# Moving the bias of three attention layers from TensorE to VectorE in a graph network kernel

## The chip, the cores and the metric

The kernel runs on one core of one Trainium2 chip. The metric is device time in microseconds for one execution, the median of several runs. The core has five engines that run their own instruction queues and wait for each other by semaphores: TensorE (PE in the profile; PEld is its loading of weights), VectorE (DVE), ScalarE (ACT), GpSimd (POOL) and SyncE (SP), which here only starts transfers.

## The reference

There are 50000 nodes with 128 features and 12500 edges, sorted by target. Two blocks follow each other: one convolution over the edges, then four attention layers, of which each does, with `x` the rows of the nodes:

```python
def _gat_layer(x, src, dst, ea, W, We, a_s, a_d, a_e, b, g, beta):
    h = x @ W
    e = ea @ We
    alpha = h @ a_s
    alpha = alpha[src] + (h @ a_d)[dst] + e @ a_e
    alpha = jax.nn.leaky_relu(alpha, NEG_SLOPE)
    alpha = _segment_softmax(alpha, dst, N)
    out = jax.ops.segment_sum(h[src] * alpha[:, None], dst, num_segments=N) + b
    mu = out.mean(-1, keepdims=True)
    var = ((out - mu) ** 2).mean(-1, keepdims=True)
    return (out - mu) * jax.lax.rsqrt(var + LN_EPS) * g + beta
...
for l in range(L):          # L = 4
    x = _gat_layer(x, src_f, dst_f, ea_f, W[l], We[l], att_src[l], ...)
```

A node without an incoming edge has only its own loop, so its row needs no other row. The kernel treats such rows apart ("dense" work) from those that edges touch.

## The kernel before, in words

Everything is fp32 unless said. The program is a sequence of blocks; in each, every engine has its own list, and all engines meet at the end of a block. After the set-up and a convolution block, four pairs follow: a dense block (`dense`, the rows no edge touches) and `attention(l)` for l = 0 to 3. The diff touches the second block of `attention`, for l = 0, 1, 2; the last layer (`final`) keeps its way of working. It also touches the set-up.

The attention block for a layer works over the edges, 125 at a time, two such groups (columns of `S` and `T`) to a **unit**: `NU` = 50 units. `S` holds the rows of the sources, `T` those of the targets, both [125, 100 or 101, 130]: 128 features and two score columns. For unit n, with ring place r = n % 4:

- `mask` (VectorE) multiplies the 0/1 matrices `M` by the attention weights into `MA`; `diagonal` (GpSimd) does the same with the identity into `DGB`. `diagonal(n)` may start when `aggregate(n-4)` is done.
- `aggregate` (TensorE) sums `S` rows by `MA` and `T` rows by `DGB` into bank r (8 passes, since an fp32 product is two passes). `copy_t` (ScalarE) takes the result to `XT`.
- `turn` (TensorE) transposes the two `S` tiles into bank 4+r (2 passes); `copy_s` (VectorE) takes them to `XT`.
- `multiply_t` and `multiply_s` (TensorE): a product of three rows of bf16 (`BR`, the bias split into three parts) with ones, 260 columns, puts the bias into the bank (L1698), and two fp32 products with the layer's weights, 130 columns, 4 passes, are added to it (L1702).
- `squares` (ScalarE) reads the rows from the banks and sums their squares, `root` takes the square root, `invert` (VectorE) the reciprocal, and `rescale_t`, `rescale_s` (VectorE, L1811 and L1818) multiply the rows in the banks by it and write them to `T` and `S`.
- `edge` (VectorE) keeps two columns of a unit for the rows that span two groups.

The order on an engine is written by hand: for slot t = 0 to 54, the operations of the list run one after the other, each for unit t minus its lag. SyncE stores ten pieces of `T` as their units get ready.

Of the kernel before, what the change touches and what calls it, by code (L numbers as in the profile page):

```python
# [11 lines left out]
D = 128  # L12
# [20 lines left out]
def gnn_kernel(nc, x, src, dst, ea, ew, w0, b0, wg, we, att_s, att_d, att_e, bg, gamma, beta, out):  # L33
    ctx = ExitStack()
    with ctx:
# [73 lines left out]
        BR = sb("BR", [3, L + 1, W], BF16)  # L109
        GC = sb("GC", [D, L])  # L110
# [513 lines left out]
        with nc.Block() as block:  # L624
# [7 lines left out]
            def _(dve):  # L632
# [18 lines left out]
                ch.add(nc.vector.tensor_copy(WIS[:, :], banks[6][0:P, 0:C]))  # L651
                dve.wait_ge(s_tab, 1)
# [71 lines left out]
            def _(pe):  # L724
                seg = segbox[0]
                carries(pe, seg, [(0, ("total", run[:, :])), (1, ("spread", lg[:, :]))])
                pe.wait_ge(s_vt, 1)
# [98 lines left out]
        def dense(first_group, groups, moves, move, arrive):  # L826
# [10 lines left out]
                "turned2_copied", "beta_added")  # L837
# [397 lines left out]
        def conv_layer():  # L1235
# [5 lines left out]
                "residual_added", "beta_added", "counted2", "variance2", "root2", "inverse2", "scale2",  # L1241
# [293 lines left out]
        def attention(l):  # L1535
# [80 lines left out]

            (masked, diag_ready, gathered, agg_copied, edged, agg_done, turned, turned_copied, next_done, squared,
# [10 lines left out]
            with nc.Block() as block:  # L1628
# [44 lines left out]
                def _(pe):  # L1673
                    def aggregate(n):
                        pe.wait_ge(*masked.at(n + 1))
                        pe.wait_ge(*diag_ready.at(n + 1))
                        r = n % NS
                        if n >= NS:
                            pe.wait_ge(*t_ready.at(n - NS + 1))
                        for a in range(2):  # L1680
                            o = banks[r][:, a * P:(a + 1) * P]
                            nc.tensor.matmul(o, S[:, 2 * n + a, 0:D], MA[:, r, a, :], start=True, stop=False,  # L1682
                                             skip_group_check=True)
                            ins = nc.tensor.matmul(o, T[:, 2 * n + a, 0:D], DGB[:, r, a, :], start=False, stop=True,  # L1684
                                                   skip_group_check=True)
                        ins.then_inc(gathered.s, 1)

                    def turn(n):
                        r = n % NS
                        if n >= NS:  # L1690
                            pe.wait_ge(*s_ready.at(n - NS + 1))
                        transposes(banks[4 + r], [S[:, 2 * n + a, 0:D] for a in range(2)]).then_inc(turned.s, 1)

                    def multiply(bank, xt, copied, done):
                        def op(n):
                            r = n % NS
                            pe.wait_ge(*copied.at(n + 1))
                            nc.tensor.matmul(product(banks[bank + r], 2 * P), ones3[:, 0:P],  # L1698
                                             BR[:, l:l + 1, 0:cols].broadcast_to([3, 2, cols]), start=True, stop=False,
                                             skip_group_check=True)  # L1700
                            for a in range(2):
                                ins = nc.tensor.matmul(product(banks[bank + r], 2 * P)[:, a, :],  # L1702
                                                       XT[:, r, xt + a * P:xt + (a + 1) * P], WCX[:, l, 0:cols],
                                                       start=False, stop=True, skip_group_check=True)
                            ins.then_inc(done.s, 1)
                        return op

                    multiply_t, multiply_s = multiply(0, 0, agg_copied, agg_done), multiply(4, 2 * P, turned_copied, next_done)
                    for t in slots:
                        run_slot(t, NU, [(0, aggregate), (1, multiply_t)] if final else [(0, turn), (0, aggregate), (1, multiply_t), (0, multiply_s)])  # L1710
# [13 lines left out]
                def _(act):  # L1724
# [8 lines left out]
                    def squares(n):  # L1733
                        r = n % NS
                        act.wait_ge(*agg_done.at(n + 1))
                        for a in range(2):
                            ins = nc.scalar.activation(Y[:, r, a, :], product(banks[r], 2 * P)[:, a, 0:D], ACT.Square,  # L1737
                                                       scale=D ** -0.5, accum_out=ss4[:, r, a:a + 1])
                        if not final:
                            act.wait_ge(*next_done.at(n + 1))  # L1740
                            for a in range(2):
                                ins = nc.scalar.activation(Y[:, r, 2 + a, :], product(banks[4 + r], 2 * P)[:, a, 0:D],
                                                           ACT.Square, scale=D ** -0.5, accum_out=ss4[:, r, 2 + a:3 + a])
# [8 lines left out]
                    for t in slots:  # L1752
                        run_slot(t, NU, [(3, root), (1, copy_t), (2, squares)])
# [8 lines left out]
                def _(dve):  # L1762
# [27 lines left out]

                    def invert(n):
# [4 lines left out]
                    def rescale_t(n):  # L1796
# [14 lines left out]
                        nc.vector.tensor_tensor(T[:, 2 * n:2 * n + 2, :], product(banks[r], 2 * P),  # L1811
# [3 lines left out]
                    def rescale_s(n):  # L1815
                        r = n % NS
                        dve.wait_ge(*inverted.at(n + 1))
                        nc.vector.tensor_tensor(S[:, 2 * n:2 * n + 2, :], product(banks[4 + r], 2 * P),  # L1818
# [3 lines left out]
                    for t in slots:  # L1822
                        run_slot(t, NU, [(0, diagonal), (0, mask), (4, rescale_t), (3, invert), (1, edge)] if final else [(0, mask), (4, rescale_s), (4, rescale_t), (0, copy_s), (3, invert), (1, edge)])
# [24 lines left out]
            for sig in (turned, turned_copied, next_done, s_ready):  # L1848
# [34 lines left out]
```

## Time and profile before

| | us |
|---|---|
| median of 3 runs (lowest, highest) | 2285.7 (2283.72, 2287.53) |
| the profiled execution, its own time | 2294.79 |
| its span, first to last instruction | 2293.1 |
| PE busy | 1745.7 (76%) |
| DVE busy | 1609.0 (70%) |
| ACT busy | 1513.0 (66%) |
| POOL busy | 1151.3 (50%) |

No engine is busy for the whole span, since the blocks differ. What a change inside one block is worth has to be read from that block: which engine has no gap there, and what the others wait for. In a timeline row the first number is the start in us from the span's start, the second how long the row's instructions took; what stands in brackets is how long the engine had been idle and what released it. Records of one engine can overlap a little, since an instruction's start is taken while the one ahead drains: the distance from one start to the next (the **pitch** below) is what an instruction costs on a full engine. A row of busy time by stretch has the stretch and its length, then for PE, PEld, DVE, ACT and POOL the busy time with the number of instructions, then TensorE's granted clock (1.00 is 2.4 GHz, 0.50 is 1.2 GHz), the share of the DMA engines and GB/s.

### The profile page before, as it was taken

The numbers are of one execution on the slowest core, as the hardware profiler recorded it, in microseconds if no ns is written. First come the engines' busy times: TensorE is split into PE (matmuls) and PEld (weight loads), VectorE is DVE, ScalarE is ACT, GpSimd is POOL, SyncE is SP. The second block draws the span as 40 slices with busy tenths as digits, with TensorE's granted clock in tenths as the row PEclk, the third lists the DMA queues.
The fourth block names the chain that finished last, engine by engine and source line by source line (L and its number), as shares of the span: only waits on it lengthen the run. The fifth ranks groups of instructions, "written<-read, shape, count | busy, mean of one in ns | idle before, by whom it ended". The sixth has DMA issues, their size and how long they took to land. (4 is left out here: it accounts for less than half of the span.)

```text
span 2293.1 us, 41415 instructions
## 1 busy us (share of the span) xinstructions
PE 1745.7 (76%) x9894; PEld 1277.6 (56%) x9894; DVE 1609.0 (70%) x8473; ACT 1513.0 (66%) x7686; POOL 1151.3 (50%) x1069
## 2 busy tenths in 40 slices
PE   2589488888488867866996875996884997884960
PEld 1589355554377764535884544884543885552850
DVE  3671699998599967975555985555995555895860
ACT  0452499999399967963665982665992664993640
POOL 0577777300155538771216772215773224774677
PEclk9995599999599977987996996996995997996985
DMA  7123323221212122212113212113113113123421
GB/s 141 24 51 84 93 78 95 76 64 32 80 51 65 51 64 60 60 46 71 47 47 75 56 42 70 47 47 84 42 46 81 40 45 91 33 51 92 107 70 35
DMA packets 123138, 145.24 MB, mean 63 GB/s; under 512 B 56197, under 2 KB 83637, under 8 KB 122145
## 3 DMA queue, kind: packets, MB, share of 16 engines
q1 hardware_dynamic: 66303, 116.40, 18.6%
q0 software_dynamic: 56160, 25.40, 5.5%
q8 instruction: 81, 1.33, 0.2%
q14 instruction: 162, 1.33, 0.2%
q10 hardware_dynamic: 432, 0.79, 0.1%
HBM read 94.60 MB, written 67.86 MB: 71 GB/s over the span
## 5 line engine op out<-in xcount | busy, mean ns | idle before, releaser
L211 POOL DMA_INDIRECT S<-row_t,rowI x400 | 541.1, 1353 | 232.2 <-issue 232.2
L938 PE MATMUL bank<-AC,XT 128*125 128x390 f32 x800 | 331.6, 521 | 0.4
L1002 ACT ACTIVATE R<-bank 125x128 f32<-125x128 f32 x1200 | 322.8, 305 | 0.0
L1656 POOL TENSOR_TENSOR R<-ident,aselfS 125x250 f32<-125x250 f32 x150 | 90.7, 607 | 391.2 <-PE bank L1684 313.8
L1002 ACT ACTIVATION_READ_ACCUMULATOR R<-bank 125x1 f32 x1200 | 277.1, 239 | 0.0
L1702 PE MATMUL bank<-WCX,XT 128*125 128x130 f32 (+1 forms) x1400 | 250.8, 302 | 0.0
L199 PE MATMUL bank<-ident,Y 125*128 125x125 f32 x800 | 130.8, 289 | 113.4 <-ACT Y L953 58.7
L199 PEld LDWEIGHTS bank<-ident,Y 125*128 125x128 f32 x800 | 98.1, 150 | 213.7 <-issue 139.0
L1789 DVE COPY XT<-bank 128x250 f32<-128x250 f32 x150 | 62.8, 418 | 210.4 <-PE bank L199 210.4
L1702 PEld LDWEIGHTS bank<-WCX,XT 128*125 128x125 f32 x1400 | 182.7, 189 | 43.4 <-issue 1.6
L1044 DVE BATCH_NORM_STATS2 st<-R 125x6 f32<-125x128 f32 x800 | 173.7, 282 | 30.5 <-issue 30.1
L211 POOL DMA_INDIRECT S<-in_x,srcI x100 | 129.7, 1297 | 111.3 <-issue 111.3
L1737 ACT ACTIVATE Y<-bank 125x128 f32<-125x128 f32 x400 | 107.2, 273 | 99.9 <-PE bank L1702 99.9
L918 PEld LDWEIGHTS bank<-AC,XT 128*125 128x125 f32 x800 | 106.2, 205 | 117.5 <-ACT SB L1019 116.2
L918 PE MATMUL bank<-AC,XT 128*125 128x128 f32 x800 | 125.1, 303 | 58.4 <-ACT SB L1019 57.7
L1682 PE MATMUL bank<-R,S 125*128 125x125 f32 x800 | 160.2, 283 | 3.9 <-DVE R L1767 2.9
L1731 ACT ACTIVATE XT<-bank 128x250 f32<-128x250 f32 x200 | 76.0, 380 | 130.0 <-PE bank L1684 130.0
L215 POOL DMA_INDIRECT out_rows<-T,repNI x101 | 123.6, 1224 | 73.1 <-DVE T L1808 42.2
L938 PEld LDWEIGHTS bank<-AC,XT 128*125 128x125 f32 x800 | 134.7, 198 | 45.5 <-ACT XT L986 8.6
L1684 PE MATMUL bank<-R,T 125*128 125x125 f32 x800 | 159.1, 281 | 0.0
L211 POOL DMA_INDIRECT T<-in_x,dstI x101 | 137.6, 1363 | 41.0 <-issue 41.0
L1024 ACT ACTIVATE R<-bank 125x128 f32<-125x128 f32 x400 | 107.9, 312 | 39.1 <-PE bank L922 37.9
(418 smaller groups left out, 5173.1 us busy)
## 6 DMA issues: line engine op xcount, KB each, us to landing
row_t<-T SPq DMA_DIRECT2D x40, 568.8 KB
R<-in_x SPq DMA_DIRECT2D x100, 224.0 KB
out_rows<-R SPq DMA_DIRECT2D x100, 224.0 KB
R<-m_t SPq DMA_DIRECT2D x5, 2734.4 KB
S<-row_t,rowI POOLq DMA_INDIRECT x400
T<-in_edge_attr SPq DMA_DIRECT2D x1, 5600.0 KB
x_t<-XB SPq DMA_DIRECT2D x50, 112.0 KB
R<-x_t SPq DMA_DIRECT2D x25, 224.0 KB
```

What stands on the lines that cost most here:

```text
L199: ins = nc.tensor.transpose(ps[:, a * P:(a + 1) * P], t, ident[0:P, 0:P])
L211: pool.indirect_dma_start(to, None, table, bass.IndirectOffsetOnAxis(ap=idx, axis=0), bounds_check=rows - 1, oob_is_err=False).then_inc(do ...
L215: pool.indirect_dma_start(table, bass.IndirectOffsetOnAxis(ap=idx, axis=0), frm, None, bounds_check=rows - 1, oob_is_err=False).then_inc(d ...
L918: nc.tensor.matmul(last_of(g)[:, a, :], h0(g, a), AC[3], start=a == 0, stop=False, skip_group_check=True)
L938: nc.tensor.matmul(LAYERS[a][0:P, 0:3 * D + 6], h0(g, a), ACB[:, 0:3 * D + 6], start=True, stop=True).then_inc(layers_done.s, 1)
L1002: ins = nc.scalar.activation(JUNK[:, a * 3 + l, :], LAYERS[a][0:P, l * D:(l + 1) * D], ACT.Square, scale=D ** -0.5, accum_out=NRM[:, g % N ...
L1024: ins = nc.scalar.activation(JUNK[:, 12 + a, :], last_of(g)[:, a, :], ACT.Square, scale=D ** -0.5, accum_out=ss4[:, g % NS, a:a + 1])
L1044: ins = nc.vector.bn_stats(ring[:, a, :], v[:, a, :])
L1682: nc.tensor.matmul(o, S[:, 2 * n + a, 0:D], MA[:, r, a, :], start=True, stop=False, skip_group_check=True)
L1684: ins = nc.tensor.matmul(o, T[:, 2 * n + a, 0:D], DGB[:, r, a, :], start=False, stop=True, skip_group_check=True)
L1702: ins = nc.tensor.matmul(product(banks[bank + r], 2 * P)[:, a, :], XT[:, r, xt + a * P:xt + (a + 1) * P], WCX[:, l, 0:cols], start=False, ...
L1737: ins = nc.scalar.activation(Y[:, r, a, :], product(banks[r], 2 * P)[:, a, 0:D], ACT.Square, scale=D ** -0.5, accum_out=ss4[:, r, a:a + 1])
```

## The change

For l = 0, 1, 2: TensorE no longer puts the bias in the banks (the fp32 products start with a clear bank), VectorE adds the bias from a new tile `BB` (the bias rows on all partitions, made once in the set-up) while it takes the products out of the banks into `T` and `S`; ScalarE squares those rows; the two scalings read and write `T` and `S`. The banks come free after the adding instead of after the scaling. The lists of slots are new.

```diff
+        BB = sb("BB", [P, L - 1, W])
...
                 ch.add(nc.vector.tensor_copy(WIS[:, :], banks[6][0:P, 0:C]))
+                dve.wait_ge(s_bc, 3)
+                ch.link(nc.vector.tensor_copy(BB[:, :, :], banks[5][0:P, 0:(L - 1) * W]
+                                              .rearrange("p (l f) -> p l f", l=L - 1)))
...
+                nc.tensor.matmul(banks[5][0:P, 0:(L - 1) * W].rearrange("p (l f) -> p l f", l=L - 1), ones3[:, 0:P],
+                                 BR[:, 0:L - 1, :], start=True, stop=True).then_inc(s_bc, 1)
...
+            bias_t, bias_s = signal("addend_added", "score_kept")
...
                     def aggregate(n):
-                            pe.wait_ge(*t_ready.at(n - NS + 1))
+                            pe.wait_ge(*(t_ready if final else bias_t).at(n - NS + 1))
                     def turn(n):
-                            pe.wait_ge(*s_ready.at(n - NS + 1))
+                            pe.wait_ge(*bias_s.at(n - NS + 1))
                     def multiply(bank, xt, copied, done):
...
-                            nc.tensor.matmul(product(banks[bank + r], 2 * P), ones3[:, 0:P],
-                                             BR[:, l:l + 1, 0:cols].broadcast_to([3, 2, cols]), start=True, stop=False,
-                                             skip_group_check=True)
+                            if final:
+                                nc.tensor.matmul(product(banks[bank + r], 2 * P), ones3[:, 0:P],
+                                                 BR[:, l:l + 1, 0:cols].broadcast_to([3, 2, cols]), start=True,
+                                                 stop=False, skip_group_check=True)
...
-                                                       start=False, stop=True, skip_group_check=True)
+                                                       start=not final, stop=True, skip_group_check=True)
...
-                        run_slot(t, NU, [(0, aggregate), (1, multiply_t)] if final else [(0, turn), (0, aggregate), (1, multiply_t), (0, multiply_s)])
+                        run_slot(t, NU, [(0, aggregate), (1, multiply_t)] if final else [(4, multiply_s), (4, multiply_t), (3, aggregate), (0, turn)])
...
                     def squares(n):
+                            act.wait_ge(*bias_t.at(n + 1))
...
+                            v = product(banks[r], 2 * P)[:, a, 0:D] if final else T[:, 2 * n + a, 0:D]
...
-                        run_slot(t, NU, [(3, root), (1, copy_t), (2, squares)])
+                        run_slot(t, NU, [(4, squares), (2, copy_t), (4, root)])
...
+                    def add_bias_t(n):
+                        dve.wait_ge(*agg_done.at(n + 1))
+                        nc.vector.tensor_tensor(T[:, 2 * n:2 * n + 2, :], product(banks[n % NS], 2 * P),
+                                                BB[:, l:l + 1, :].broadcast_to([P, 2, W]), ALU.add).then_inc(bias_t.s, 1)
+
+                    def add_bias_s(n):
+                        dve.wait_ge(*gathered.at(n + 1))
+                        dve.wait_ge(*next_done.at(n + 1))
+                        nc.vector.tensor_tensor(S[:, 2 * n:2 * n + 2, :], product(banks[4 + n % NS], 2 * P),
+                                                BB[:, l:l + 1, :].broadcast_to([P, 2, W]), ALU.add).then_inc(bias_s.s, 1)
...
-                        nc.vector.tensor_tensor(T[:, 2 * n:2 * n + 2, :], product(banks[r], 2 * P),
+                        nc.vector.tensor_tensor(T[:, 2 * n:2 * n + 2, :], T[:, 2 * n:2 * n + 2, :],
                                                 rr4[:, r, 0:2].unsqueeze(2).broadcast_to([P, 2, W]),
...
-                        nc.vector.tensor_tensor(S[:, 2 * n:2 * n + 2, :], product(banks[4 + r], 2 * P),
+                        nc.vector.tensor_tensor(S[:, 2 * n:2 * n + 2, :], S[:, 2 * n:2 * n + 2, :],
                                                 rr4[:, r, 2:4].unsqueeze(2).broadcast_to([P, 2, W]),
...
-                        run_slot(t, NU, [(0, diagonal), (0, mask), (4, rescale_t), (3, invert), (1, edge)] if final else [(0, mask), (4, rescale_s), (4, rescale_t), (0, copy_s), (3, invert), (1, edge)])
+                        run_slot(t, NU, [(0, diagonal), (0, mask), (4, rescale_t), (3, invert), (1, edge)] if final else [(0, mask), (1, add_bias_s), (0, copy_s), (1, add_bias_t), (2, edge), (3, invert), (5, rescale_t), (3, rescale_s)])
```

TensorE's list in the middle of the first attention layer, one slot, before. L199 is the transposing, L1682 and L1684 the aggregation, L1698 the bias, L1702 the product with the layer's weights; in brackets the semaphores waited for (`turned1_copied` is ScalarE's copy_t, `turned2_copied` VectorE's copy_s).

```order
L199 MATMUL bank<-ident,S 128x125 [waits s_rows_ready]
L1682 MATMUL bank<-R,S 128x125 [waits t_rows_ready,diagonal_ready,masked]
L1684 MATMUL bank<-R,T 128x125
L1682 MATMUL bank<-R,S 128x125
L1684 MATMUL bank<-R,T 128x125
L1698 MATMUL bank<-BR,ones 125x260 [waits turned1_copied]
L1702 MATMUL bank<-WCX,XT 125x130 x2
L1698 MATMUL bank<-BR,ones 125x260 [waits turned2_copied]
```

The same place of the changed kernel. Its lines 200, 1689 and 1691, 1710 are those of the transposing, the aggregation and the product.

```order
L200 MATMUL bank<-ident,S 128x125 [waits score_kept]
L1710 MATMUL bank<-WCX,XT 125x130 [waits turned2_copied]
L1710 MATMUL bank<-WCX,XT 125x130
L1710 MATMUL bank<-WCX,XT 125x130 [waits turned1_copied]
L1710 MATMUL bank<-WCX,XT 125x130
L1689 MATMUL bank<-R,S 128x125 [waits addend_added,diagonal_ready,masked]
L1691 MATMUL bank<-R,T 128x125
```

Both bias products are gone; the products now stand ahead of the next aggregation, `multiply_s` first, and the banks are waited for through the adding (`addend_added`, `score_kept`) instead of through the scaled rows.

VectorE's list at the same place, one slot, before: masks L1767, scaling L1818 and L1811, copy_s L1789, invert L1794, edge L1780.

```order
L1767 TENSOR_TENSOR R<-R,alphaS 125x250 [waits aggregated]
L1818 TENSOR_TENSOR S<-bank,rr 125x260 [waits inverse1]
L1811 TENSOR_TENSOR T<-bank,rr 125x260 [waits inverse1]
L1789 COPY XT<-bank 128x250 [waits score_ready,turned2]
L1794 RECIPROCAL rr<-rt 125x4 [waits root1]
L1780 COPY EDGE<-XT 128x4 [waits turned1_copied]
```

And of the changed kernel: mask L1779, add_bias_s L1811, copy_s L1801, add_bias_t L1805, edge L1792, invert L1817, rescale_t L1834, rescale_s L1841.

```order
L1779 TENSOR_TENSOR R<-R,alphaS 125x250 [waits aggregated]
L1811 TENSOR_TENSOR S<-bank,BB 125x260 [waits score_ready,aggregated]
L1801 COPY XT<-bank 128x250 [waits score_ready,turned2]
L1805 TENSOR_TENSOR T<-bank,BB 125x260 [waits conv_done]
L1792 COPY EDGE<-XT 128x4 [waits turned1_copied]
L1817 RECIPROCAL rr<-rt 125x4 [waits root1]
L1834 TENSOR_TENSOR T<-T,rr 125x260 [waits inverse1]
L1841 TENSOR_TENSOR S<-S,rr 125x260 [waits inverse1]
```

Two instructions are new in each slot, and the scalings, which had a bank as their first operand, now have two operands that are both in the on-chip memory, and stand right ahead of the next mask, which has two such operands too.

## Rows read from the trace of the kernel before

**Rows 1.** The page: busy time of each engine over the span

```profile
PE 1745.7 (76%) x9894; PEld 1277.6 (56%) x9894; DVE 1609.0 (70%) x8473; ACT 1513.0 (66%) x7686; POOL 1151.3 (50%) x1069
```

**Rows 2.** Busy time by stretch: start of first attention block, its middle, a dense block

```profile
1054.00:1062.00 8.00, 7.50 (x29) 6.25 (x30) 2.42 (x6) 0.76 (x2) 3.82 (x6) 0.50 0.01 3
1063.00:1200.00 137.00, 137.00 (x953) 113.99 (x951) 73.23 (x284) 87.51 (x477) 26.40 (x44) 1.00 0.14 44
450.00:500.00 50.00, 43.45 (x214) 26.06 (x215) 50.00 (x306) 50.00 (x294) 0.00 (x0) 1.00 0.22 63
```

**Rows 3.** Timeline of TensorE, one slot in the middle of the first attention block

```profile
1071.68 0.38 PE L199 MATMUL bank<-ident,S 125*128 125x125 f32 x2
1071.90 0.39 PE L1682 MATMUL bank<-R,S 125*128 125x125 f32 x2
...
1072.88 0.32 PE L1698 MATMUL bank<-BR,ones 3*125 3x260 bf16 x1
1073.13 0.71 PE L1702 MATMUL bank<-WCX,XT 128*125 128x130 f32 x4
1073.77 0.32 PE L1698 MATMUL bank<-BR,ones 3*125 3x260 bf16 x1
1074.02 0.71 PE L1702 MATMUL bank<-WCX,XT 128*125 128x130 f32 x4
1074.57 0.38 PE L199 MATMUL bank<-ident,S 125*128 125x125 f32 x2
```

**Rows 4.** Timeline of VectorE, the same slot

```profile
1072.10 0.42 DVE L1789 COPY XT<-bank 128x250 f32<-128x250 f32 x1 [1.33 <-PE bank L199]
1072.43 0.17 DVE L1794 RECIPROCAL rr<-rt 125x4 f32<-125x4 f32 x1
1072.51 0.14 DVE L1780 COPY EDGE<-XT 128x4 f32<-128x4 f32 x1
1072.56 0.41 DVE L1767 TENSOR_TENSOR R<-R,alphaS 125x250 f32<-125x250 bf16 x1
1072.89 0.42 DVE L1818 TENSOR_TENSOR S<-bank,rr 125x260 f32<-125x260 f32 x1
1073.23 0.42 DVE L1811 TENSOR_TENSOR T<-bank,rr 125x260 f32<-125x260 f32 x1
```

**Rows 5.** Timeline of ScalarE and of GpSimd, the same slot, behind the aggregation

```profile
1072.99 0.38 ACT L1731 ACTIVATE XT<-bank 128x250 f32<-128x250 f32 x1 [0.52 <-PE bank L1684]
...
1073.03 0.60 POOL L1656 TENSOR_TENSOR R<-ident,aselfS 125x250 f32<-125x250 f32 x1 [2.28 <-PE bank L1684]
```

**Rows 6.** Timeline, start of the first attention block: GpSimd, VectorE and TensorE

```profile
1054.22 0.59 POOL L1656 TENSOR_TENSOR R<-ident,aselfS 125x250 f32<-125x250 f32 x1 [23.97 <-POOLq L1541]
...
1054.78 0.77 POOL L1656 TENSOR_TENSOR R<-ident,aselfS 125x250 f32<-125x250 f32 x1
...
1054.23 0.87 DVE L1767 TENSOR_TENSOR R<-R,alphaS 125x250 f32<-125x250 bf16 x1 [0.30 <-PEq L1541]
...
1055.15 0.79 PE L1682 MATMUL bank<-R,S 125*128 125x125 f32 x2 [0.27 <-DVE R L1767]
```

**Rows 7.** Timeline of the convolution block: GpSimd, and VectorE's scale operation twice

```profile
704.10 0.68 POOL L1284 TENSOR_TENSOR R<-T,Y 125x256 f32<-125x256 f32 x1
...
704.38 0.42 DVE L1442 SCALAR_TENSOR_TENSOR nm<-mv,rr 125x4 f32<-125x4 f32 x1
...
707.70 0.15 DVE L1442 SCALAR_TENSOR_TENSOR nm<-mv,rr 125x4 f32<-125x4 f32 x1
```

**Rows 8.** Timeline of VectorE in the last layer's attention block

```profile
2153.12 0.43 DVE L1808 TENSOR_TENSOR T<-T,R 125x256 f32<-125x256 f32 x1
2153.46 0.16 DVE L1794 RECIPROCAL rr<-rt 125x2 f32<-125x2 f32 x1
```

**Rows 9.** Timeline, end of the first attention block: first square and last scaling of unit 49

```profile
1202.61 0.28 ACT L1737 ACTIVATE Y<-bank 125x128 f32<-125x128 f32 x1 [0.30 <-PE bank L1702]
...
1204.67 0.42 DVE L1811 TENSOR_TENSOR T<-bank,rr 125x260 f32<-125x260 f32 x1
```

More of the change, by code:

```diff
@@ L836, in dense @@
                 "variance2", "root2", "inverse2", "scale2", "rows2_vector", "rows2_scalar", "turned2",
-                "turned2_copied", "beta_added")
+                "turned2_copied", "addend_added")
             (layers_done, normed, first_sum, s1_ready, mixed1, mixed2, second_sum, s2_ready, mixed3, mixed4, third_sum,
@@ L1240, in conv_layer @@
                 "aggregated", "turned1_copied", "conv_done", "slope_ready", "leaky_done", "edge_columns_kept",
-                "residual_added", "beta_added", "counted2", "variance2", "root2", "inverse2", "scale2",
+                "residual_added", "addend_added", "counted2", "variance2", "root2", "inverse2", "scale2",
                 "rows2_scalar", "turned2", "turned2_copied", "score_ready", "score_kept")
@@ L1734, in squares @@
                         r = n % NS
-                        act.wait_ge(*agg_done.at(n + 1))
+                        if final:
+                            act.wait_ge(*agg_done.at(n + 1))
+                        else:
+                            act.wait_ge(*bias_t.at(n + 1))
                         for a in range(2):
-                            ins = nc.scalar.activation(Y[:, r, a, :], product(banks[r], 2 * P)[:, a, 0:D], ACT.Square,
-                                                       scale=D ** -0.5, accum_out=ss4[:, r, a:a + 1])
+                            v = product(banks[r], 2 * P)[:, a, 0:D] if final else T[:, 2 * n + a, 0:D]
+                            ins = nc.scalar.activation(Y[:, r, a, :], v, ACT.Square, scale=D ** -0.5,
+                                                       accum_out=ss4[:, r, a:a + 1])
                         if not final:
-                            act.wait_ge(*next_done.at(n + 1))
+                            act.wait_ge(*bias_s.at(n + 1))
                             for a in range(2):
-                                ins = nc.scalar.activation(Y[:, r, 2 + a, :], product(banks[4 + r], 2 * P)[:, a, 0:D],
-                                                           ACT.Square, scale=D ** -0.5, accum_out=ss4[:, r, 2 + a:3 + a])
+                                ins = nc.scalar.activation(Y[:, r, 2 + a, :], S[:, 2 * n + a, 0:D], ACT.Square,
+                                                           scale=D ** -0.5, accum_out=ss4[:, r, 2 + a:3 + a])
                         ins.then_inc(squared.s, 1)
@@ L1847, in attention @@
                 sig.base += NU
-            for sig in (turned, turned_copied, next_done, s_ready):
+            for sig in (turned, turned_copied, next_done, s_ready, bias_t, bias_s):
                 sig.base += 0 if final else NU
```

## The prediction

> **What bounds the kernel now.** I read the page first: no engine is busy for more than 76% of the span [rows 1], so nothing is said by the whole, and the change must be costed inside the blocks it touches. The busy time by stretch shows the middle of the first attention block (137 us): TensorE is busy for all of it, at the full granted clock, VectorE for 73 of 137 us and ScalarE for 88 [rows 2]. The timeline of one slot says the same from the other side: VectorE does its six instructions back to back and then sits idle for 1.33 us until TensorE's transposing is done [rows 4], ScalarE waits 0.52 us for the aggregation, and GpSimd 2.28 us [rows 5]. So this block is TensorE's, and its slot is the distance from one L199 to the next, 1074.57 - 1071.68 = 2.89 us [rows 3]; VectorE's, from 1072.10 to 1073.65 and 1.33 idle, is 2.88 [rows 4]; I use 2.885. A block is 50 such slots; the first ones run at half clock, about 8 us [rows 2].
>
> **Inside a TensorE slot.** From the starts [rows 3]: two transposing passes take 0.22; the aggregation, eight passes at 0.11, and what comes before the bias product, 0.98, of which 8 x 0.111 = 0.89 are the passes and 0.09 is a gap; a bias product takes 0.25 until L1702 starts; L1702 takes 0.64 until the next bias product and 0.55 until the transposing. A pass of 130 columns should last 130/125 of 0.111, that is 0.115, so four last 0.46, and the rest of L1702's distances (0.18 and 0.09) is gap again. All gaps stand at bias products: between other fp32 passes there is none, although they wait on semaphores too. Passes alone are 0.22 + 0.89 + 2 x 0.46 = 2.03 us a slot, and the two bias products with their gaps 2.885 - 2.03 = 0.855.
>
> **The change part by part.**
>
> TensorE: what is removed is worth between 2 x 0.25 = 0.50 (gaps stay) and 0.855 us a slot (gaps go). I take 0.855, because the gaps stand only there: its slot falls to 2.03 (at most 2.385), if nothing else is waited for.
>
> VectorE: pitches before are copy_s 0.33, invert 0.08, edge 0.05, mask 0.33, rescale_s 0.34, rescale_t 0.34 (the last as the one before), sum 1.47 [rows 4]. Two additions of 260 columns with a bank as operand are like the scalings of before, 0.34 each. The scalings of after read the on-chip memory in place of a bank: the like instruction in the last layer (two such operands, 256 columns) has a pitch of 0.34 too [rows 8], so nothing changes by that. Sum: 1.47 + 0.68 = 2.15 us. VectorE would be the longest engine, by 0.12 over TensorE.
>
> GpSimd against VectorE: this is the term that decides. At the start of the block GpSimd's `diagonal` starts at 1054.22 and the mask, which reads two tiles of the on-chip memory, at 1054.23: it takes 0.87 instead of 0.41, 0.46 longer [rows 4, 6]. In the convolution block a VectorE instruction of 4 columns with two such operands takes 0.42 instead of 0.15, when it starts 0.28 into a GpSimd instruction of 0.68 [rows 7]: it was held until 704.38 + 0.42 - 0.15 = 704.65, 0.13 before that one's end. In the middle of the block nothing is held: the scalings run beside `diagonal` (1073.03 to 1073.63) with one operand in a bank, at their usual 0.42 [rows 4, 5]. After the change both scalings are of the kind that is held, and one hold is 0.60 - 0.13 = 0.46 to 0.47 us. Does the one `diagonal` of a slot meet them? Let a mask start at m. In VectorE's new order, add_s is at m + 0.33, copy_s + 0.67, add_t + 1.00, edge + 1.34, invert + 1.39, rescale_t + 1.47, rescale_s + 1.81, next mask + 2.15. TensorE, the faster one, waits for that mask: from the mask's end to the start of the aggregation is 0.05 [rows 6], the weights of a product that had to wait load in about 0.1, the aggregation is 0.89, and GpSimd starts 0.24 after its last pass (72.79 to 73.03) [rows 3, 5]. So `diagonal` asks at m + 0.41 + 0.05 + 0.10 + 0.89 + 0.24 = m + 1.69, inside rescale_t, and right behind that stands rescale_s, of the same kind. No row shows what happens between two such instructions. Bounds: GpSimd gets its turn there, and rescale_s is held by 0.46 (slot 2.61); or VectorE keeps it through rescale_s and the mask, `diagonal` runs beside add_s and copy_s, whose other operand is a bank, and nothing is held (slot 2.15), since `diagonal` is due three slots later only. I take 2.61: GpSimd has then been waiting for 0.1 us when rescale_s comes, and at the block's start the waiting mask got in ahead of GpSimd's own next instruction, which took 0.77 instead of 0.60 [rows 5, 6]. The phase is stable: TensorE still waits for the mask (2.03 + 0.15 of lost loading and handing over is under 2.61), so `diagonal` asks at the same place each time.
>
> The Trainium skill, "SBUF — State Buffer", section "Who interferes with whom", has the rule for this pair: a VectorE instruction with two inputs in SBUF contends with a GpSimd instruction that reads SBUF, and the second fully blocks until the first is done. With a hold of GpSimd's whole 0.60 us the slot would be 2.75. The mask's 0.46 [rows 6] says it is a little less than the whole.
>
> Waits that are new: add_s(n) stands ahead of copy_s(n+1), edge and mask, all of which TensorE needs. With a slot of 2.61 multiply_s(n) is over 2.61 - 0.56 - 0.89 - 0.22 - 0.46 = 0.48 before the mask starts, so add_s at m + 0.33 does not wait. `turn(n+4)` waits for add_s(n), done at m + 0.8, and is reached at m + 1.45. copy_t(n+1) starts at m + 1.65 and takes 0.38 [rows 5]; multiply_t(n+1) is reached at m + 2.13. All are covered, the last by some 0.1.
>
> ScalarE: it was busy for 88 of 137 us, 1.84 a slot [rows 2]; its squares read other places and are not more. 1.84 is under 2.61 and under 2.15. Cost nothing.
>
> Ends of a block: unit 49 before went from the first square to the end of the last scaling in 1205.09 - 1202.61 = 2.48 [rows 9]. After, an addition (0.42 + 0.03) comes ahead, and two more scalings between invert and the last one, since rescale_t lags by five slots (0.68); against that TensorE has no lone slot for multiply_t(49). I put the ends at +0.35 a block. Half-clock part: no change, +0. Set-up: one bf16 product and one VectorE copy of 390 columns, which its next instruction waits for; nearest is the copy of 250 columns at 0.42 [rows 4], so 0.7 us, between 0 and 1.2.
>
> **The sum**, against the profiled execution (span 2293.1, own time 2294.8, 9.1 over the median of the runs shown): 48 slots at full clock x (2.885 - 2.61) = 13.2, less 0.35, is 12.9 a block; three blocks 38.5; less 0.7 is 37.8. Span after 2255; taken from the median of 2285.7 it is 2248.
>
> **Rivals.**
>
> *VectorE is never held.* Slot 2.15: (48 x 0.735 - 0.35) x 3 - 0.7 = 104, time 2182. For it: no row shows GpSimd getting between two adjoining VectorE instructions, and `diagonal` asks only some 0.1 before rescale_s. Against it: the waiting engine got in at the block's start.
>
> *The hold is longer, or falls on VectorE with the whole 0.60.* Slot 2.75: (48 x 0.135 - 0.35) x 3 - 0.7 = 18, time 2268.
>
> *Scaling from the on-chip memory is cheaper than from a bank.* VectorE's two scalings would each save up to half of the difference in fixed cost; what rows show is 0.413 us for the mask, 250 columns with both operands there, and 0.42 for a copy of 250 columns from a bank [rows 4]: under 0.01. With both at the pitch of TensorE's floor and no hold the slot is 2.03: 121 us, time 2165. The Trainium skill, "VectorE: DVE Perf Modes", section "The TRN2 errata — SBUF-src ops pay a fixed extra latency per instruction", has 58 cycles of fixed cost from SBUF and 120 from PSUM, 0.065 us less for each scaling; by it, as an estimate, a held slot would be 2.48 and the time some 19 us under mine. The rows do not bear it out.
>
> *Slower: TensorE falls to 1.2 GHz because it now waits in each slot.* At half clock the 2.03 us of passes are 4.06, 1.18 more than before: (48 x 1.18 + 0.35) x 3 + 0.7 = 172 us, time 2457, if all slots fell. It decides from a small part on: a half-clock slot costs 1.45 more than one of 2.61, so 26 of the 144 slots take all of the gain. Against it: in a dense block TensorE is busy for 43.5 of 50 us, with waits, at a granted clock of 1.00 [rows 2], and the new slot has TensorE at work for 2.03 + 0.1 of 2.61 us, 82%, with more matmuls in a microsecond (18 in 2.61 against 214 in 50).
>
> *The gain is not there,* since handing over between VectorE and TensorE makes a ring of the same length as before: the ring of multiply_s, add_s, and on to the mask and the aggregation is worked out above with slack, so this has little.
>
> **How the numbers follow.** Held once: 0.52. Never held (with or without cheaper scaling): 0.27. Hold of 0.6 or somewhat more: 0.08. No change: 0.05. Slower by the clock or a ring I did not see: 0.08. Forecast 2248. The range reaches from 2176, a little under the never-held case, to 2270, over the long hold, and leaves out the cases of no change and slower and the deepest of the fast ones, together under 0.2. For the likeliest case alone I would say 2238 to 2260. A measurement of this kernel tells 0.2%, 4.6 us, from no change. Faster 0.87, within 0.05, slower 0.08.
>
> **What the changed profile would show.** TensorE in the middle of the block no longer busy throughout, its wait ended by VectorE's mask at L1779; no gap between the passes of L1710 and L1691. VectorE without idle time, slot 2.61. One of rescale_t and rescale_s in each slot at about 0.88 us, the other at 0.42; `diagonal` at about 0.7 instead of 0.60. The granted clock at 1.00. If both scalings are at 0.42 and the slot is near 2.15, the second case holds. The prediction is wrong if the clock is lower in the block, if VectorE waits for TensorE or ScalarE in it, or if the additions cost more than 0.34.

## The result

The changed kernel takes 2234.8 us (2232.1 to 2236.7 in three of its four runs) against 2286.2 for the kernel before; the ratio is 0.977, 95% interval 0.975 to 0.979. The fourth run (2338.1) had a lower granted clock and is left out of the comparison. Forecast were 2248 and a range of 2176 to 2270. The gain, some 51 us by the medians and 58 between the two profiled executions (spans 2293.1 and 2234.9), is larger than the 38 I had summed, and comes from the place and the mechanism forecast.

The page after, busy time of the engines and, under it, TensorE's granted clock in 40 slices, against [rows 1]:

```profile
PE 1663.9 (74%) x9595; PEld 1239.8 (55%) x9595; DVE 1751.1 (78%) x8774; ACT 1496.0 (67%) x7686; POOL 1154.6 (52%) x1069
...
PEclk9995599999689996996996996996996996995985
```

TensorE is busy for 82 us less, VectorE for 142 more. Time in which an instruction is held counts as busy, so of the 142 some 3 x 40 x 0.40 = 48 us are no work; the rows below show where they lie. The stretch in the middle of the first attention block, which answers to the second of [rows 2] (the columns are the same):

```profile
1066.00:1180.00 114.00, 104.59 (x813) 96.05 (x811) 113.68 (x361) 78.99 (x459) 27.33 (x43) 1.00 0.15 47
```

VectorE, 73 of 137 us before, is now busy for all of it, TensorE for 105 of 114, and its clock stays at the full level. One slot of VectorE, from mask to mask, against [rows 4], and under it GpSimd's instruction in that slot, against [rows 5]:

```profile
1102.69 0.41 DVE L1779 TENSOR_TENSOR R<-R,alphaS 125x250 f32<-125x250 bf16 x1
1103.02 0.42 DVE L1811 TENSOR_TENSOR S<-bank,BB 125x260 f32<-125x260 f32 x1
1103.36 0.40 DVE L1801 COPY XT<-bank 128x250 f32<-128x250 f32 x1
1103.68 0.41 DVE L1805 TENSOR_TENSOR T<-bank,BB 125x260 f32<-125x260 f32 x1
1104.02 0.15 DVE L1792 COPY EDGE<-XT 128x4 f32<-128x4 f32 x1
1104.09 0.16 DVE L1817 RECIPROCAL rr<-rt 125x4 f32<-125x4 f32 x1
1104.17 0.39 DVE L1834 TENSOR_TENSOR T<-T,rr 125x260 f32<-125x260 f32 x1
1104.49 0.82 DVE L1841 TENSOR_TENSOR S<-S,rr 125x260 f32<-125x260 f32 x1
1105.23 0.41 DVE L1779 TENSOR_TENSOR R<-R,alphaS 125x250 f32<-125x250 bf16 x1
...
1104.39 0.64 POOL L1663 TENSOR_TENSOR R<-ident,aselfS 125x250 f32<-125x250 f32 x1 [1.91 <-PE bank L1691]
```

Read the starts: a slot is 1105.23 - 1102.69 = 2.54 us. Edge and invert have a pitch of 0.07 and 0.08, every other instruction one of 0.32 to 0.34, except rescale_s, L1841: 0.74, and 0.82 long. GpSimd's diagonal started 0.10 ahead of it, inside rescale_t. TensorE's row after that, against [rows 3], shows who it waits for:

```profile
1105.69 0.49 PE L1689 MATMUL bank<-R,S 125*128 125x125 f32 x2 [0.21 <-DVE R L1779]
```

It starts 0.46 after the start of the mask, and TensorE had been idle for 0.21 us, waiting for that mask. The last three slots of the block are the control that the program carries with itself, since GpSimd has made its last diagonal by then (VectorE, columns as above):

```profile
1178.19 0.41 DVE L1779 TENSOR_TENSOR R<-R,alphaS 125x250 f32<-125x250 bf16 x1
...
1179.99 0.41 DVE L1841 TENSOR_TENSOR S<-S,rr 125x260 f32<-125x260 f32 x1
1180.33 0.41 DVE L1779 TENSOR_TENSOR R<-R,alphaS 125x250 f32<-125x250 bf16 x1
```

There rescale_s takes 0.41, and the slot is 2.14.

### The profile page after: what moved, and what is told of

Read it like the earlier page. It is cut to its first block and busy times, and to the rows that moved or that the text cites. A ratio compares the mean times of both kernels' runs of the same rounds, so it can differ in the third digit from the quotient of the medians.

```text
span 2234.9 us, 41269 instructions
## 1 busy us (share of the span) xinstructions
PE 1663.9 (74%) x9595; PEld 1239.8 (55%) x9595; DVE 1751.1 (78%) x8774; ACT 1496.0 (67%) x7686; POOL 1154.6 (52%) x1069
## 5 line engine op out<-in xcount | busy, mean ns | idle before, releaser
L1663 POOL TENSOR_TENSOR R<-ident,aselfS 125x250 f32<-125x250 f32 x150 | 95.3, 637 | 333.7 <-PE bank L1691 257.8
L1710 PE MATMUL bank<-WCX,XT 128*125 128x130 f32 (+1 forms) x1400 | 210.2, 289 | 2.6 <-ACT XT L1739 2.4
L1689 PE MATMUL bank<-R,S 125*128 125x125 f32 x800 | 174.3, 300 | 33.9 <-DVE R L1779 27.6
L1689 PEld LDWEIGHTS bank<-R,S 125*128 125x128 f32 x800 | 124.6, 196 | 62.0 <-DVE R L1779 51.7
L207 PE MATMUL bank<-W,R 128*125 128x128 f32 x800 | 129.7, 311 | 0.0
```

What stands on the lines that cost most here:

```text
L207: ins = nc.tensor.matmul(pz[0:P, a, :], xt[:, a * P:(a + 1) * P], w, start=False, stop=True, skip_group_check=True)
```

## The experiments

The theory: TensorE's bias products cost some 0.86 us a slot; without them VectorE's list sets the slot at 2.14, and GpSimd's diagonal adds 0.40 to it by holding the scaling of S. The rivals: the scaling is slow by itself; the gain is due to the new lists. The kernel before, timed again beside these kernels, took 2289 to 2291 us at the median. A ratio and its 95% interval are given where a kernel was run several times; a time without a ratio is a single run. Single runs are read by their slots, which repeat to 0.01 us, more than by their times: the start of the first attention block alone lies anywhere between 1050.2 and 1057.4 us in the nine kernels that have the same code ahead of it.

**Scalings behind the mask.**

```diff
-[(0, mask), (1, add_bias_s), (0, copy_s), (1, add_bias_t), (2, edge), (3, invert), (5, rescale_t), (3, rescale_s)]
+[(0, mask), (5, rescale_t), (4, rescale_s), (1, add_bias_s), (0, copy_s), (1, add_bias_t), (2, edge), (3, invert)]
```

> VectorE's list of the changed kernel in another order: mask, rescale_t, rescale_s (now with lag 4), add_s, copy_s, add_t, edge, invert. Nothing else. Theory (GpSimd's diagonal holds the scaling that stands in its way): diagonal asks some 1.7 us after the mask's start, which is now add_t, with a bank as operand, so all scalings take about 0.39 to 0.42, the slot falls from 2.54 to 2.14 us and the time by 3 x 44 x 0.40 = 53 us, to about 2182. Rival (the scaling of S is slow by itself, right behind the other or close to the reciprocal it reads): it stays at 0.82, the slot at 2.54, the time at 2235.

Measured 2201.7, ratio 0.962 (0.960 to 0.965). Both scalings were down to 0.41 and 0.42, so the rival falls, but the slot was 2.30 and not 2.14. The timeline of that kernel shows the new place of the hold, first GpSimd, then VectorE:

```profile
1102.26 0.60 POOL L1663 TENSOR_TENSOR R<-ident,aselfS 125x250 f32<-125x250 f32 x1 [1.70 <-PE bank L1691]
...
1102.57 0.32 DVE L1792 COPY EDGE<-XT 128x4 f32<-128x4 f32 x1
1102.80 0.16 DVE L1817 RECIPROCAL rr<-rt 125x4 f32<-125x4 f32 x1
1102.89 0.38 DVE L1779 TENSOR_TENSOR R<-R,alphaS 125x250 f32<-125x250 bf16 x1
```

Edge copies four columns within the on-chip memory, with one input, and takes 0.32 instead of 0.15: it ends with diagonal, 1102.89 against 1102.86. My theory had only instructions with two such inputs in it. It was too narrow.

**No diagonal that reads.**

```diff
+                        if n >= NS:
+                            nc.gpsimd.memset(little[:, n:n + 1], 0.0).then_inc(diag_ready.s, 1)
+                            return
...
```

> The changed kernel, but GpSimd makes the diagonal matrices only for the first four units of each of the three layers; for the others it writes 125 numbers instead, and the products use the matrices that lie there, so the self loops of those units get wrong weights. Theory of the hold: with no GpSimd instruction that reads, rescale_s takes 0.41 and the slot is 2.14, the time about 2182. Rival, that the scaling is slow by itself: 0.82 and 2.54 as before, 2235.

Measured 2180.2. VectorE's rescale_s (L1845 there) and the masks around it:

```profile
1100.07 0.41 DVE L1783 TENSOR_TENSOR R<-R,alphaS 125x250 f32<-125x250 bf16 x1
...
1101.87 0.42 DVE L1845 TENSOR_TENSOR S<-S,rr 125x260 f32<-125x260 f32 x1
1102.21 0.41 DVE L1783 TENSOR_TENSOR R<-R,alphaS 125x250 f32<-125x250 bf16 x1
```

Same list, same place, 0.42 and a slot of 2.14: it is GpSimd's instruction that makes the difference. What it has in its place is both without a read and much smaller, so this run by itself doesn't tell which of the two matters; the run with one wait more, below, keeps the instruction whole.

**The kernel before without bias products.**

```diff
                         def op(n):
...
+                            if final:
                                 nc.tensor.matmul(product(banks[bank + r], 2 * P), ones3[:, 0:P],
...
-                                                       start=False, stop=True, skip_group_check=True)
+                                                       start=not final, stop=True, skip_group_check=True)
```

> The kernel before, with the bias products of the first three layers left out and nothing put in their place (the bias is missing in those layers). It shows what they cost TensorE. Theory: the gaps of 0.09 and 0.18 stand only at them and go too: slot 2.03 to 2.06 us instead of 2.885, unless the mask or copy_s comes late; time about 2286 - 3 x 48 x 0.84 = 2165. Rival: the gaps belong to the changes from aggregation to product and stay: slot 2.385, time about 2214.

Measured 2152.0. TensorE from one transposing to the next:

```profile
1099.34 0.38 PE L199 MATMUL bank<-ident,S 125*128 125x125 f32 x2
...
1100.45 1.05 PE L1703 MATMUL bank<-WCX,XT 128*125 128x130 f32 x8
1101.34 0.38 PE L199 MATMUL bank<-ident,S 125*128 125x125 f32 x2
```

2.00 us against 2.89: 0.885 a slot, 0.44 for each bias product of 260 columns. The gaps went with them; the eight passes of L1703 run on in 1101.34 - 1100.45 = 0.89. The rows of TensorE's weight loads say what the gaps were: between fp32 passes a load starts 0.11 ahead of its pass (1072.46 for the pass at 1072.57 in the kernel before), but the loads for L1698 and for the L1702 behind it start only with their products, at 1072.88 and 1073.13. This is also TensorE's floor, which no version below reaches, for they all carry VectorE's additions.

**Bias on both engines.**

```diff
-                            if final:
+                            if True:
                                 nc.tensor.matmul(product(banks[bank + r], 2 * P), ones3[:, 0:P],
...
-                                                       start=not final, stop=True, skip_group_check=True)
+                                                       start=False, stop=True, skip_group_check=True)
```

> The changed kernel with TensorE's bias products put back as well, so the bias is added twice in the first three layers. Theory (all of the gain is TensorE's, 0.885 us a slot by the run without bias products): TensorE is the longest engine again with 2.89 a slot, VectorE's new work and the hold disappear in its idle time, time about 2285 to 2290. Rival (part of the gain is from the new lists or from banks that come free earlier): under 2270.

Measured 2285.8, where the seven runs of the kernel before beside it lie between 2282.4 and 2299.4: all of the gain is gone, with the new lists and the early freed banks in place. VectorE's work is still longer, and diagonal now meets another instruction, but it costs nothing (GpSimd, then VectorE):

```profile
1120.54 0.77 POOL L1663 TENSOR_TENSOR R<-ident,aselfS 125x250 f32<-125x250 f32 x1 [2.12 <-PE bank L1691]
...
1119.61 0.43 DVE L1805 TENSOR_TENSOR T<-bank,BB 125x260 f32<-125x260 f32 x1
...
1120.42 0.42 DVE L1841 TENSOR_TENSOR S<-S,rr 125x260 f32<-125x260 f32 x1
1120.76 0.82 DVE L1779 TENSOR_TENSOR R<-R,alphaS 125x250 f32<-125x250 bf16 x1
...
1122.49 0.43 DVE L1805 TENSOR_TENSOR T<-bank,BB 125x260 f32<-125x260 f32 x1
```

The mask is held to 0.82, but the slot is 1122.49 - 1119.61 = 2.88, which is TensorE's. GpSimd waits here too: it asks 0.12 into rescale_s, and takes 0.77 instead of 0.60.

**New work in the old lists.**

```diff
-[(4, multiply_s), (4, multiply_t), (3, aggregate), (0, turn)]
+[(0, turn), (0, aggregate), (1, multiply_t), (0, multiply_s)]
-[(4, squares), (2, copy_t), (4, root)]
+[(3, root), (1, copy_t), (2, squares)]
-[(0, mask), (1, add_bias_s), (0, copy_s), (1, add_bias_t), (2, edge), (3, invert), (5, rescale_t), (3, rescale_s)]
+[(0, mask), (4, rescale_s), (4, rescale_t), (1, add_bias_s), (0, copy_s), (3, invert), (1, add_bias_t), (1, edge)]
```

> The changed kernel's operations in lists like those of the kernel before (TensorE turn, aggregate, multiply_t with lag 1, multiply_s; VectorE mask, rescale_s and rescale_t with lag 4, add_s with lag 1, copy_s, invert, add_t with lag 1, edge). Theory: the ring mask, aggregation (0.05 + 0.1 + 0.89), multiply_t (0.46), hand over 0.2, add_t, edge, next mask is 0.41 + 1.04 + 0.46 + 0.2 + 0.34 + 0.05 = 2.50 us, and diagonal meets add_s or copy_s, which it does not hold: slot about 2.50, time about 2230, the new lists being no gain by themselves. Rival: the new lists are what makes the gain possible, and with the old ones the slot stays near 2.88, time about 2280.

Measured 2229.3, slot 2.52 in all the middle of the block. The row that ends the ring, VectorE:

```profile
1101.44 0.43 DVE L1805 TENSOR_TENSOR T<-bank,BB 125x260 f32<-125x260 f32 x1 [0.27 <-PE bank L1710]
```

VectorE waits for TensorE's product before add_t, and TensorE waits for the next mask: no engine is full, nothing is held (both scalings 0.42), and the slot is the ring's length, forecast at 2.50. The new lists of the change remove this ring, and pay for it with the hold, 0.40: as they stand they gain nothing over the old ones. From the first mask of the first block to its last are 124.6 us in this kernel and 124.4 in the changed one; that the times are 5.5 us apart is no sign for the old lists, since the first block of this one starts 5.6 us earlier.

**Scalings swapped.**

```diff
-[(0, mask), (1, add_bias_s), (0, copy_s), (1, add_bias_t), (2, edge), (3, invert), (5, rescale_t), (3, rescale_s)]
+[(0, mask), (1, add_bias_s), (0, copy_s), (1, add_bias_t), (2, edge), (3, invert), (4, rescale_s), (4, rescale_t)]
```

> The changed kernel with the two scalings swapped at their place: invert, rescale_s (lag 4), rescale_t (lag 4), mask. Theory: diagonal gets its turn after the first of the two, whichever it is, so now rescale_s takes about 0.42 and rescale_t 0.8, slot 2.54, time 2235. Rival (the S rows are the slow ones): rescale_s keeps 0.82.

Measured 2237.2, slot 2.54. VectorE, then GpSimd:

```profile
1120.69 0.39 DVE L1841 TENSOR_TENSOR S<-S,rr 125x260 f32<-125x260 f32 x1
1121.01 0.82 DVE L1834 TENSOR_TENSOR T<-T,rr 125x260 f32<-125x260 f32 x1
...
1120.91 0.64 POOL L1663 TENSOR_TENSOR R<-ident,aselfS 125x250 f32<-125x250 f32 x1 [1.91 <-PE bank L1691]
```

Now T is the slow one: the place decides, not the tile. GpSimd's instruction started while the first ran, took 0.64 instead of 0.60, and got in ahead of the second, although that one follows without a gap.

**Edge moved, then edge and invert moved.** Two kernels on the way to 2.14. The first line is the list with edge moved, the second that with invert moved too:

```diff
+[(0, mask), (5, rescale_t), (4, rescale_s), (2, edge), (1, add_bias_s), (0, copy_s), (1, add_bias_t), (3, invert)]
...
+[(0, mask), (5, rescale_t), (5, rescale_s), (2, edge), (4, invert), (1, add_bias_s), (0, copy_s), (1, add_bias_t)]
```

> The order with the scalings right behind the mask, in which the slot was 2.30 and not 2.14 because edge (128 by 4 elements copied within the on-chip memory) took 0.32 instead of 0.15 and ended with diagonal; here edge too stands ahead of the additions: mask, rescale_t, rescale_s, edge, add_s, copy_s, add_t, invert. Theory (edge was held by diagonal although it has one input only): edge takes 0.15, slot 2.14, time about 3 x 44 x 0.16 = 21 us under that kernel, 2180; if invert, now in edge's place, is held as edge was, the slot stays near 2.30. Rival (edge was waiting for ScalarE's copy, or is slow by itself): it stays at 0.32, 2.30, 2201.

> As the one before it, and invert too ahead of the additions (lag 4; rescale_s lag 5): mask, rescale_t, rescale_s, edge, invert, add_s, copy_s, add_t. Nothing between the additions and the next mask can be held by diagonal, which ends its hold at about the mask's start. Theory: slot 2.14, time about 2180, the same as the one before if invert isn't held, 20 us under it if invert is. Rival: the mask is now held by what is left of diagonal, 2.2 to 2.3.

Measured 2191.4 (ratio 0.956, 0.953 to 0.959) and 2191.3 (0.956, 0.953 to 0.959). Edge is back at 0.16, so the wait was diagonal's, and invert takes 0.16 in the first of them although diagonal runs beside it. But the slots alternate between 2.18 and 2.29 in the first and between 2.24 and 2.29 in the second: 2.14 was missed, and what I had called the rival is what happens, in the second kernel (GpSimd, then VectorE):

```profile
1122.13 0.60 POOL L1663 TENSOR_TENSOR R<-ident,aselfS 125x250 f32<-125x250 f32 x1 [1.69 <-PE bank L1691]
...
1122.44 0.56 DVE L1779 TENSOR_TENSOR R<-R,alphaS 125x250 f32<-125x250 bf16 x1
```

The mask is now what diagonal holds, at 0.56 instead of 0.41: if its own work takes the usual 0.41, that begins at 1122.44 + 0.56 - 0.41 = 1122.59, 0.14 before diagonal's end.

**One wait more for GpSimd.** If the hold is a matter of when diagonal asks, the list can stay, and diagonal be put where VectorE reads banks:

```diff
                         if n >= NS:
                             pool.wait_ge(*gathered.at(n - NS + 1))
+                            pool.wait_ge(*masked.at(n - 2))
```

> The changed kernel with one more wait on GpSimd and nothing else: diagonal(n) also waits for mask(n - 3), so it asks some 0.46 us after the start of a mask and not 1.7, when VectorE is at add_s and copy_s, which read a bank. Theory of the hold: rescale_s 0.42, slot 2.14 to 2.15, time 3 x 44 x 0.40 = 53 us under the changed kernel, 2182. Rival (what is gained at one place is given back, since TensorE waits for the mask or the adding in another order): slot 2.2 to 2.3, 2190 to 2203.

Measured 2180.2, ratio 0.9525 (0.950 to 0.955): the interval lies wholly under that of the changed kernel, about 56 us faster by the two ratios (0.0246 of 2290). The same place of the list, VectorE and GpSimd:

```profile
1119.61 0.40 DVE L1780 TENSOR_TENSOR R<-R,alphaS 125x250 f32<-125x250 bf16 x1
...
1121.09 0.38 DVE L1835 TENSOR_TENSOR T<-T,rr 125x260 f32<-125x260 f32 x1
1121.41 0.41 DVE L1842 TENSOR_TENSOR S<-S,rr 125x260 f32<-125x260 f32 x1
1121.75 0.40 DVE L1780 TENSOR_TENSOR R<-R,alphaS 125x250 f32<-125x250 bf16 x1
...
1120.15 0.60 POOL L1664 TENSOR_TENSOR R<-ident,aselfS 125x250 f32<-125x250 f32 x1 [1.54 <-DVE R L1780]
```

Diagonal is released by the mask and runs, as long as ever, beside add_s and copy_s; rescale_s takes 0.41, the slot 2.14. The first block takes 114.5 us against 131.2 in the changed kernel and 150.9 in the one before.

**The other list, with diagonal timed.**

```diff
+                        if n >= 7:
+                            pool.wait_ge(*inverted.at(n - 6))
...
+[(0, mask), (5, rescale_t), (5, rescale_s), (2, edge), (4, invert), (1, add_bias_s), (0, copy_s), (1, add_bias_t)]
```

> The list mask, rescale_t, rescale_s, edge, invert, add_s, copy_s, add_t, whose slot was 2.24 to 2.30 with the mask at 0.51 to 0.56, and GpSimd's diagonal(n) waiting for invert(n - 7) too, so that it asks when add_s starts and is over before the next mask. Theory (what was left of the slot over 2.14 is the mask held by the end of diagonal): mask 0.41, slot 2.14, time some 3 x 44 x 0.12 = 16 us under that kernel, 2175. Rival (it is TensorE, which waits for add_s before the next turn): slot stays at 2.24 or over, 2191.

Measured 2182.3, ratio 0.953 (0.9505 to 0.955); slot 2.14, mask 0.40. The part over 2.14 was the hold, not TensorE's wait for the adding. With diagonal out of the way both lists come to the same time, so the rearranging was not needed.

## Why the prediction was right, and what was off

The measured 2234.8 lies in the range, 13 us under the forecast of 2248, and 3 us under the 2238 to 2260 that I had given for the likeliest case alone. So the case was the one forecast, and its price was too small; what follows says in which terms.

The bound of before: right. TensorE's slot fell by 0.885 when the bias products were taken out and nothing put in, and the gain was gone when they were put back.

TensorE's term: taken at 0.855 with the gaps, between 0.50 and 0.855; measured 0.885, a little outside, since the passes of 130 columns are 0.11 and not 0.115. No part of the gain hangs on it, for TensorE no longer sets the slot.

VectorE's list: 2.15 summed, 2.14 measured, in four kernels. The additions have the pitch of the scalings they stand beside (0.33 to 0.34). Scaling from the on-chip memory: 0.32 and 0.34 of pitch, against 0.34 from a bank. The rule of the Trainium skill, "VectorE: DVE Perf Modes", section "The TRN2 errata — SBUF-src ops pay a fixed extra latency per instruction", from which I had worked out 0.065 us less for each, is not borne out: it was 0 to 0.02.

The hold: right in place, in which instruction, in who is released first, and in its being steady. Diagonal was to ask 1.69 after the mask's start, and does at 1104.39 - 1102.69 = 1.70. The signs were somewhat off: a slot of 2.54 and not 2.61, rescale_s at 0.82 and not 0.88, diagonal at 0.64 and not 0.7. They are off for one reason. The hold was put at 0.46, with GpSimd's work beginning when rescale_s starts; it is 0.40. Diagonal takes only 0.04 longer than its 0.60, so by this its work begins at 1104.43, 0.06 ahead of rescale_s's start, and the rest is as forecast: if rescale_s's own work takes 0.41 to 0.42, it begins about 0.13 before diagonal's recorded end. The Trainium skill's rule for the pair, "SBUF — State Buffer", section "Who interferes with whom", agrees with what rescale_s, rescale_t and the mask showed. The same section names a copy in a two-port mode as a second kind of instruction that contends, and edge is a copy with one input, and was held; whether it ran in such a mode no run shows. I had left that kind out.

What the sum had too small is seen in the block, 150.86 before and 131.17 after, 19.7 less where I had 12.9. From the starts of the masks: the first six slots are 2.1 us shorter, the next 40 are 0.34 shorter each (13.6, where 0.275 would give 11.0), the last three 0.74 shorter each (2.2), since there is no diagonal left to hold anything, and the end of the block is 1.7 shorter.

Against the sum, which had 48 of the 50 slots at 0.275 each and +0.35 for the ends, that is 2.6 too little for the size of the hold, 1.4 for the last three slots, about 1.0 for the beginning and 1.8 for the end. So the two terms that were off are the hold (0.46 for 0.40, and counted in all 48 slots where the last three have none) and the ends of the block. At the end, the stretch that I had priced, from the first square of unit 49 to the end of the last scaling, did get longer, from 2.48 to 3.14 (1183.94 to 1187.08); but the stretch ahead of it, from the last mask to that square, fell from 5.98 to 3.61. That fits what I had named and left without a price, that TensorE has less to do there; the end of the block was not tested by itself. Three blocks at 19.7, less the later start of the first, are 57.4 of the 58.2 us between the two profiled executions.

The beginning goes with TensorE's clock: it rose to full about 4.7 us after the block's start (the start of its first mask), before the change only at 7.8. Granted clock of two stretches, the first of the kernel before, the second after (the column ahead of the last two numbers), both of one us and some 5 to 7 us behind the start of the block:

```profile
1060.00:1061.00 1.00, 1.00 (x6) 0.78 (x4) 0.05 (x1) 0.06 (x1) 0.01 (x1) 0.50 0.00 0
```

```profile
1061.00:1062.00 1.00, 1.00 (x11) 1.00 (x11) 0.91 (x3) 0.07 (x1) 0.03 (x1) 1.00 0.00 0
```

An estimate from these: 3.1 us less at half clock is 1.5 us of TensorE's work, most of the 2.1. It is the same in the other two blocks, 7.9 and 7.7 before, 4.5 and 4.2 after. But the new list of TensorE (it begins with three transposings in a row) is not what brings the early rise: with the new work in the old lists the rise came at 4.5, 4.2 and 4.8, and with the new lists and the bias on both engines at 4.9, 4.8 and 9.1. In the last layer, whose code is the same in both kernels, it came at 4.3 before and 6.7 after. What decides it stays open, and so this part of the gain was not foreseeable from the rows.

Set-up: VectorE's copy into BB takes 0.55, but right behind it VectorE waits for TensorE 0.61 instead of 1.21, and is as far behind the kernel before as it was ahead of the copy, 0.7. So the 0.7 put in for it is not borne out at that place. The first block starts 1.7 later than before, which says nothing of the set-up: that start differs by up to 7.3 between kernels with the same code ahead of it.

The rivals: never held (2182) was wrong for this kernel, and its time is what came out, 2180, once diagonal was moved. Slower by the clock: no, 1.00 at 92% busy. A ring as long as before: not in the new lists; in the old ones there is a ring, of 2.52.

## What to carry to other kernels

When an instruction gets a second operand in the on-chip memory, or is a plain copy within it, look for GpSimd instructions that read there at the same time: here one of 0.60 us cost VectorE 0.40 in each slot as soon as VectorE was the full engine, and nothing while it had idle time. Before rearranging the full engine's list, try to move the other engine's instruction by one more wait: it gave as much as the change itself. And price a small product by what its place takes from the row of large ones: 260 columns of three rows cost 0.44 us here, of which 0.25 was in plain sight.

## What the runs showed of the hardware that I had not expected

A copy of 128 by 4 elements within the on-chip memory, one input, is held by a GpSimd instruction that runs (0.32 instead of 0.15), while a reciprocal of 125 by 4 elements beside the same instruction took its usual 0.16. GpSimd gets in between two VectorE instructions that follow each other without a gap, when it has asked during the first, 0.10 and 0.22 ahead of the second's start in the rows above. It pays 0.04 for it in one case and 0.17 in the other (0.64 and 0.77 for 0.60). Both ways the turn passes about 0.13 before the recorded end of the instruction that has it, if the held one's own work takes its usual time: VectorE to GpSimd at 1104.43 (rescale_t ends at 1104.56) and at 1120.71 (rescale_s ends at 1120.84), GpSimd to VectorE at 1104.90 or so (diagonal ends at 1105.03). A bf16 product among fp32 ones costs 0.19 us more than the time to the next instruction's start shows (0.44 against 0.25): the weights for it and for the fp32 product behind it were not loaded ahead (1072.88 and 1073.13 for both the load and the product).
